# Triangle planes stored by halves of the picture, T loaded for two tiles in one DMA of 128 partitions, and the turned picture kept in bands

## The chip, the core and the metric

The kernel runs on one core of a Trainium2 chip. TensorE (PE) multiplies matrices into PSUM, VectorE (DVE), ScalarE (ACT) and GpSimd (POOL) work elementwise, and SyncE (SP) issues DMAs between DRAM and SBUF (128 partitions); ScalarE issues some DMAs too. One DMA is spread over the core's 16 DMA engines. The metric is the device time of one execution in microseconds, as the median of several runs; lower is better.

## The reference

The input x is a picture of 192 x 192 pixels with 64 channels in f32. Four layers follow one another, each of this form:

```python
def _L1_conv_ref(z, mask, ...):
    x = _layernorm(z, ln_in_w, ln_in_b)                      # layer 3 has none
    a = m * sigmoid(x @ w_a_g + b_a_g) * (x @ w_a_p + b_a_p)
    b = m * sigmoid(x @ w_b_g + b_b_g) * (x @ w_b_p + b_b_p)
    t = jnp.einsum('bikc,bjkc->bijc', a, b)                  # layers 0 and 1
    t = _layernorm(t, ln_out_w, ln_out_b) @ w_o + b_o
    g = sigmoid(x @ w_g + b_g)
    return g * t
```

and `x = x + layer(_gn(x))` with a group norm (32 groups over the whole picture) each time. Layers 2 and 3 contract over the other axis, `einsum('bkjd,bkid->bijd', left, right)`. Layers 0 and 2 multiply by the gate before the output matrix, layers 1 and 3 after it. Layer 0's product is made in bf16, the others in f32.

## The kernel before

**Layout.** A tile is two rows of pixels of the upper half of the picture and two of the lower: partition 64h + c holds channel c of half h, 384 pixels on the free axis. There are 48 tiles (`TILES`), taken four at a time through rings of four slots (`RING`, `TURNS` = 12).

**Stage A** (`phase_a`) normalises each tile, projects it to left and right with their gates (L568, L578), and VectorE's `glu` writes the products to `lr`, which fills most of SBUF (L1062, L1069). The gate of the output goes to DRAM (`gate_scratch`, L342). For layers 1 and 3 the tiles come from `x_scratch` one by one (`load`, L309).

**Stage B1** (`phase_b1`) multiplies left by right for 64 channels, four channels a group (`GROUPS` = 16): row i of the plane T on PSUM partitions. ScalarE copies the first 128 rows of a group to SBUF (`main`, L846) and issues their store (L850); VectorE copies the other 64 (`tail`, L1113) and SP stores them in two DMAs (L380). T lies in DRAM as `t_scratch` [64 channels][192 x 192 pixels] (`t_scratch_bf16` in layer 0). Between the tails SP loads residual tiles into parts of `lr` that are free (L370), in layers 1 to 3 after a wait for ScalarE's copy. A slot of `plane_out` is used again after four groups, when `planes_stored` has counted its three DMAs.

**Stage B2** (`phase_b2`) reads T back. `load_t` brings two tiles of both halves into `in_ring`, in two DMAs of 64 partitions and 192 KB (96 KB in layer 0), L405; `centre` (L678) waits for both. Two pairs of tiles are in the ring; a new pair is issued when the two tiles of its slots have been centred (`b2_z`). Variance (L693), spreading of the deviation (L702), the output matrix (L718), the bias and the residual (L1144, or L1150 and L1277) and the group norm's statistics (L1155) follow. At the start of the stage TensorE runs filler matmuls (`keep_clock`, L618), and in layer 0 two more ahead of each of the first four output matmuls.

**The turn.** Layers 2 and 3 work on the transposed picture. At the end of layer 1 ScalarE writes each new tile transposed into `turned`, part of `lr` (L889). When all 48 are there, the whole is written to `turned_scratch` [half h][half h2][channel][96 j][96 i]: SP writes the first 8 of 96 rows j of each of the four blocks (L453, `EARLY` = 4 tiles), ScalarE the other 88 (L926), a partition's rows being 3 KB and 33 KB long without a break. SP waits for its four and then gathers the first tiles of layer 2 (`gather`, L316): one DMA of 128 partitions for each half h, for two tiles. SP keeps each gathered pair in `x_scratch` (`keep`, L321) for the residual. The second round of gathers waits for ScalarE's four DMAs (`turned_stored[1]`), for the slots to be used and for the kept pair to have landed. VectorE waits for all eight before it writes to `lr`.

**Order.** All orders are written out by hand: each engine runs its own program, and semaphores are the only ties. DMAs of a queue are issued in the order of that engine's code, and a wait in it holds back whatever stands behind it.

## Time and profile before

| | us |
|---|---|
| median of three runs | 1471.77 (1465.33 to 1473.02) |
| the profiled execution | 1468.82 |
| its span, first to last instruction | 1466.6 |

| stage | layer 0 | layer 1 | layer 2 | layer 3 |
|---|---|---|---|---|
| first gate matmul of A (L550) | 54.5 | 399.0 | 815.1 | 1163.9 |
| first and last product matmul of B1 (L636) | 246.4 to 271.2 | 576.7 to 642.0 | 975.8 to 1038.7 | 1289.7 to 1352.1 |
| first and last centring matmul of B2 (L678) | 280.4 to 373.1 | 652.2 to 746.9 | 1048.7 to 1146.2 | 1361.7 to 1455.1 |

(Starts in us from the first instruction; the last product matmul of L636 is within a us of the end of B1.) Over the span PE is busy 87%, DVE 69%, ACT 64%, POOL 36%. The times of the profile are those of one execution. A busy share is an average over stages that have different limits, so the stages are read one by one: which wait ends last there. A row of waits tells who waited, for whom, how long in all, how often, and the longest; a DMA has an issue (a time on the queue of SP, SPq, or of ScalarE, ACTq) and a landing, some us later.

### The profile page before, as it was taken

To read this page: it belongs to the slowest core of one execution; us is meant where nothing else is said; L and a number is where in the kernel's file an instruction comes from. 1 tells how busy PE (TensorE), PEld (TensorE's weight loads), DVE (VectorE), ACT (ScalarE), POOL (GpSimd) and SP (SyncE) were. 2 spreads that over 40 slices of the span, in tenths; PEclk is the share of its full clock that TensorE was granted. 3 is DMA by queue.
4 is the path that set the end of the run, shared out by engine and by line. 5 is a ranking of instruction groups with operands and counts; after the bars stand their busy time and mean duration, and the time that the engine had idled before them with its cause. 6 is when DMAs were issued, how large, how long until landed. Compare 5 with 4: busy or idle time off the path is not lost. (4 is left out here: it accounts for less than half of the span.)

```text
span 1466.6 us, 43428 instructions
## 1 busy us (share of the span) xinstructions
PE 1268.9 (87%) x12854; PEld 769.3 (52%) x12854; DVE 1006.8 (69%) x2880; ACT 932.2 (64%) x2045; POOL 528.5 (36%) x490
## 2 busy tenths in 40 slices
PE   0799998899799998999950999999899788899898
PEld 0455554577454544765530555557555343467564
DVE  6577776388699996219970788852299899921687
ACT  0577775599577774229960788851499677722675
POOL 0355552045455553004530666630055300000355
PEclk9999999999899999999985999999999899999999
DMA  8011113578433332986659455549799544469797
GB/s 286 22 50 52 50 48 97 154 221 253 155 109 107 107 112 73 285 270 188 193 147 222 153 185 165 176 136 299 243 277 282 182 154 150 145 208 312 236 300 251
DMA packets 219684, 258.74 MB, mean 176 GB/s; under 512 B 53984, under 2 KB 208992, under 8 KB 219360
## 3 DMA queue, kind: packets, MB, share of 16 engines
q1 hardware_dynamic: 185504, 227.18, 49.9%
q10 hardware_dynamic: 34112, 30.68, 7.4%
q8 instruction: 40, 0.66, 0.2%
q14 instruction: 28, 0.23, 0.1%
HBM read 139.83 MB, written 117.96 MB: 176 GB/s over the span
## 5 line engine op out<-in xcount | busy, mean ns | idle before, releaser
L1062 DVE SCALAR_TENSOR_TENSOR lr<-ps,mask,act_out 128x128 f32 (+5 forms) x1152 | 278.8, 310 | 52.9 <-ACT act_out L805 46.5
L1232 POOL TENSOR_TENSOR rstd<-ve,half_col 128x6 f32<-128x6 f32 x144 | 190.3, 1322 | 254.8 <-DVE ve L1029 221.1
L1277 POOL TENSOR_TENSOR new_ring<-val,lr 128x384 f32<-128x384 f32 x96 | 103.4, 1077 | 386.6 <-issue 303.1
L568 PE MATMUL ps<-w_parts,val 64*128 64x256 bf16 (+1 forms) x1728 | 199.1, 309 | 18.9 <-DVE lr L1062 18.1
L805 ACT ACTIVATE act_out<-ps 128x384 f32<-128x384 f32 x384 | 176.0, 483 | 50.3 <-PE ps L578 34.1
L1265 POOL TENSOR_TENSOR val<-act_out,gate_ring 128x384 f32<-128x384 f32 x96 | 103.6, 1080 | 225.1 <-ACT act_out L882 186.0
L781 ACT ACTIVATE cen<-ps,gn 128x384 f32<-128x384 f32 x144 | 83.8, 582 | 102.0 <-PE ps L523 99.6
L859 ACT ACTIVATE cen<-ps 128x384 f32<-128x384 f32 x192 | 108.5, 565 | 61.9 <-PE ps L678 61.6
L678 PE MATMUL ps<-in_ring,k 128*128 128x384 f32 x288 | 130.3, 536 | 17.5 <-DMA in_ring<-t_scratch 17.2
L1113 DVE COPY cen<-ps 128x384 f32<-128x384 f32 x48 | 26.8, 558 | 160.6 <-PE ps L636 160.6
L636 PE MATMUL ps<-lr 64*128 64x192 f32 (+3 forms) x896 | 125.5, 330 | 8.8 <-DVE lr L1062 5.2
L1239 POOL TENSOR_TENSOR rb<-rstd,one_col 128x384 f32<-128x384 f32 x144 | 128.8, 894 | 11.3
L523 PE MATMUL ps<-in_ring,w_centre 128*128 128x384 f32 x192 | 92.7, 571 | 42.9 <-issue 42.7
L568 PEld LDWEIGHTS ps<-w_parts,val 64*128 64x128 bf16 (+1 forms) x1728 | 79.2, 114 | 78.0 <-DVE lr L1062 40.9
L636 PEld LDWEIGHTS ps<-lr 64*128 64x128 f32 (+3 forms) x896 | 103.9, 179 | 27.7 <-issue 17.5
L874 ACT ACTIVATE rb<-rstd 128x384 f32<-128x384 f32 x192 | 114.4, 596 | 3.8 <-DVE rstd L1123 3.8
L1024 DVE TENSOR_TENSOR sq_low<-sq 128x384 bf16<-128x384 f32 x144 | 79.5, 552 | 54.1 <-ACT sq L783 54.1
L814 ACT ACTIVATE val<-xn 128x384 bf16<-128x384 f32 (+1 forms) x144 | 75.3, 523 | 64.8 <-PE ps L578 42.6
L797 ACT ACTIVATE gate_ring<-ps,gate_bias 128x384 f32<-128x384 f32 x192 | 111.2, 579 | 5.8 <-PE ps L550 5.5
L1132 DVE TENSOR_TENSOR xn<-ps,cen 128x384 f32<-128x384 f32 x192 | 104.4, 544 | 15.0 <-PE ps L702 12.4
L861 ACT ACTIVATE sq<-ps 128x384 f32<-128x384 f32 x192 | 106.7, 556 | 0.0
L578 PE MATMUL ps<-w_parts,val 64*64 64x128 bf16 (+1 forms) x3456 | 105.5, 235 | 0.0
(112 smaller groups left out, 2595.5 us busy)
## 6 DMA issues: line engine op xcount, KB each, us to landing
gate_scratch<-gate_ring SPq DMA_DIRECT2D x192, 192.0 KB, 2.3
gate_ring<-gate_scratch SPq DMA_DIRECT2D x96, 384.0 KB, 3.7
lr<-x_scratch SPq DMA_DIRECT2D x72, 384.0 KB, 5.1
in_ring<-t_scratch SPq DMA_DIRECT2D x144, 192.0 KB, 3.4
x_scratch<-new_ring SPq DMA_DIRECT2D x48, 384.0 KB, 3.2
in_ring<-x_scratch SPq DMA_DIRECT2D x96, 192.0 KB, 2.4
lr<-x SPq DMA_DIRECT2D x6, 1536.0 KB, 15.9
t_scratch<-cen SPq DMA_DIRECT2D x96, 96.0 KB, 4.0
```

The lines of the kernel that those rows point to most:

```text
L568: mm = nc.tensor.matmul(banks[h][:, :, 0:P], moving(x, s)[half(h), N * r:N * r + P], proj_weights(w, h)[:, 0:2 * P], start=start, stop=sto ...
L578: mm = nc.tensor.matmul(banks[h][TAIL * e:TAIL * e + TAIL, :, P:COLS], moving(x, s)[half(h), N * r + P:N * r + N], proj_weights(w, h)[:, 2 ...
L636: mm = nc.tensor.matmul(ps[:, b + i % 2, N * (i // 2):N * (i // 2) + N], left[:, 0:P], right, start=first and i < 2, stop=last and i >= 2, ...
L678: nc.tensor.matmul(ps[:, s % 2, 0:TILE], w_c, t_slots(l, s)[:, 0, :], start=True, stop=True).then_inc(b2_z, 1)
L797: nc.scalar.activation(gate_ring[:, s, :], ps[:, 3, 0:TILE], ACT.Sigmoid, bias=gate_bias[:, 0:1])\
L805: nc.scalar.activation(act_out[:, r, :].rearrange("p (h c) -> p h c", h=2), ps[:, 4 + 2 * r:6 + 2 * r, COLS:2 * COLS], ACT.Sigmoid).then_i ...
L859: nc.scalar.activation(cen[:, s, :], ps[:, s % 2, 0:TILE], ACT.Copy, scale=T_SCALE[l])\
L861: nc.scalar.activation(sq[:, s % 2, :], ps[:, s % 2, 0:TILE], ACT.Square, scale=T_SCALE[l])\
L874: nc.scalar.activation(rb[:, s % 2, :].rearrange("p (a c) -> p a c", c=C), rstd[:, s % 2, :].rearrange("p (a o) -> p a o", o=1) .broadcast ...
L1062: ins = nc.vector.scalar_tensor_tensor(out5[:, h, lo // 2:hi // 2, :, m], ps[:, 4 + 2 * r + h, lo:hi].rearrange("p (a e) -> p a e", e=2), ...
L1232: nc.gpsimd.tensor_tensor(rstd[:, s % 2, :], ve[:, s % 2, :], half_col[:, :], ALU.pow)\
L1239: nc.gpsimd.tensor_tensor(rb[:, s % 2, :].rearrange("p (a c) -> p a c", c=C), rstd[:, s % 2, :].rearrange("p (a o) -> p a o", o=1) .broadc ...
```

## The change

- T's planes lie in DRAM by halves of the picture: `t_scratch` is now [2][64 channels][96 x 192 pixels]. Half and channel together are 128 rows of equal distance, so `load_t` is one DMA of 128 partitions and 384 KB.
- A group's plane is stored in four DMAs: ScalarE stores rows 0 to 95 (96 partitions), SP the tail as before and then, after a wait for ScalarE's copy (now in every layer and group), rows 96 to 127 (32 partitions).
- The turned picture lies in DRAM in 24 bands of 8 rows j: [band][128 partitions][8 x 96], 3 KB per partition and band. SP stores the first band of each half h2 (2 DMAs of 128 partitions), ScalarE the other 11 of each (2 DMAs). A gather of two tiles is four DMAs of 64 partitions.
- In layer 0's B2 the two `keep_clock` matmuls ahead of each of the first four output matmuls are gone.
- Counts of semaphores follow.

```diff
--- before.py
+++ after.py
@@ -36,7 +36,8 @@
 TURNS = TILES // RING
 PAIRS = RING // 2
 PIECES = 6
-EARLY = 4
+BAND = 2 * RING
+BANDS = HALF // BAND
 SUBS = ROWS * TILES
 GROUP = 4
 GROUPS = C // GROUP
@@ -61,9 +62,9 @@
 def build_triangle_layers(nc, x_in, params, consts, mask3_k, mask3_row, x_out):
     scratch = nc.dram_tensor("x_scratch", [TILES, P, TILE], F32).ap()
     gate_dram = nc.dram_tensor("gate_scratch", [TILES, P, TILE], F32).ap()
-    turned_dram = nc.dram_tensor("turned_scratch", [2, 2, C, HALF, HALF], F32).ap()
-    t_f32 = nc.dram_tensor("t_scratch", [C, N * N], F32).ap()
-    t_bf16 = nc.dram_tensor("t_scratch_bf16", [C, N * N], BF16).ap()
+    turned_dram = nc.dram_tensor("turned_scratch", [2 * BANDS, P, BAND * HALF], F32).ap()
+    t_f32 = nc.dram_tensor("t_scratch", [2, C, HALF * N], F32).ap()
+    t_bf16 = nc.dram_tensor("t_scratch_bf16", [2, C, HALF * N], BF16).ap()
 
     with ExitStack() as ctx:
         def sb(name, shape, dt=F32):
@@ -184,10 +185,10 @@
         turned = lr[:, N * HALF:2 * N * HALF].rearrange("p (j i) -> p j i", i=HALF)
 
 
-        def turned_rows(h, h2, first, behind):
-
-            return (turned_dram[h, h2, :, first:behind, :],
-                    turned[C * h:C * h + C, HALF * h2 + first:HALF * h2 + behind, :])
+        def turned_bands(first, count):
+
+            bands = turned.rearrange("p (b j) i -> p b (j i)", j=BAND)
+            return (turned_dram.rearrange("b p f -> p b f")[:, first:first + count, :], bands[:, first:first + count, :])
 
         x_all = lr[:, COLS * N // 2:].rearrange("p (t f) -> p t f", f=TILE)
 
@@ -196,7 +197,7 @@
 
         def t_tiles(l, n):
 
-            return t_dram(l).rearrange("c (h t f) -> h c t f", h=2, f=TILE)[:, :, bass.ds(n, 2), :]
+            return t_dram(l).rearrange("h c (t f) -> (h c) t f", f=TILE)[:, bass.ds(n, 2), :]
 
         slots = lr[:, :].rearrange("p (a f) -> p a f", f=TILE)
 
@@ -233,15 +234,15 @@
 
         def plane_dram(l):
 
-            return t_dram(l).rearrange("(g d) (i j) -> g i d j", d=GROUP, j=N)
+            return t_dram(l).rearrange("h (g d) (i j) -> g h i d j", d=GROUP, j=N)
 
         def planes_count(l, g):
 
-            return 48 * (l * (GROUPS // RING) + g // RING)
+            return 64 * (l * (GROUPS // RING) + g // RING)
 
         def in_count(l, s=0):
 
-            return 16 * TURNS * ((l > 1) + (l > 2) * (2 if s % 2 == 0 else 0))
+            return 16 * TURNS * ((l > 1) + (l > 2) * (4 if s % 2 == 0 else 0))
 
         n_params = [4 + HAS_LN[l] + (1 if l < 2 else (2 if HAS_MASK[l] else 0)) for l in range(LAYERS)]
 
@@ -308,16 +309,18 @@
                 def load(n, s):
                     sp.dma_start(in_ring[:, s, :], src[n, :, :]).then_inc(in_loaded[s], 16)
 
-                def gather(n, s):
+                def gather(band, s):
 
                     for h in range(2):
-                        rows = turned_dram[h].rearrange("h2 c j i -> (h2 c) j i")[:, bass.ds(ROWS * n, 2 * ROWS), :]
-                        slot = in_ring[:, s:s + 2, :].rearrange("p a (r i) -> p (a r) i", r=ROWS)
-                        sp.dma_start(slot[:, :, HALF * h:HALF * h + HALF], rows).then_inc(in_loaded[s], 16)
+                        for h2 in range(2):
+                            rows = turned_dram[bass.ds(BANDS * h2 + band, 1), C * h:C * h + C, ROWS * HALF * s:ROWS * HALF * (s + 2)]
+                            slot = in_ring[C * h2:C * h2 + C, s:s + 2, :].rearrange("p a (r i) -> p (a r) i", r=ROWS)
+                            sp.dma_start(slot[:, :, HALF * h:HALF * h + HALF],
+                                         rows.rearrange("b p (r i) -> p (b r) i", i=HALF)).then_inc(in_loaded[s], 16)
 
                 def keep(n, i, s):
 
-                    sp.wait_ge(in_loaded[s], in_count(l) + 32 * (i + 1))
+                    sp.wait_ge(in_loaded[s], in_count(l) + 64 * (i + 1))
                     sp.dma_start(two_tiles(scratch, n), in_ring[:, s:s + 2, :]).then_inc(natural_stored[s // 2], 16)
 
                 def step_gathering(n, i, s, ahead):
@@ -325,7 +328,7 @@
 
                         sp.wait_ge(used, l * TILES + n + lead + 1)
                         sp.wait_ge(natural_stored[s // 2], 16 * (i + 2))
-                        gather(n + lead + RING - 1, s - 1)
+                        gather(i + 2, s - 1)
                     sp.wait_ge(a_gate, l * TILES + n + 1)
                     sp.dma_start(gate_dram[n, :, :], gate_ring[:, s, :]).then_inc(gate_stored[s], 16)
                     if s % 2 and ahead >= RING + 1:
@@ -343,15 +346,15 @@
 
                 if l == 2:
                     for n in range(0, RING, 2):
-                        gather(n, n)
+                        gather(0, n)
                     for n in range(0, RING, 2):
                         keep(n, 0, n)
 
-                    sp.wait_ge(turned_stored[1], 16 * 4)
+                    sp.wait_ge(turned_stored[1], 16 * 2)
                     for n in range(0, RING, 2):
                         sp.wait_ge(used, l * TILES + n + 2)
                         sp.wait_ge(natural_stored[n // 2], 16)
-                        gather(RING + n, n)
+                        gather(1, n)
                     keep(RING, 1, 0)
                     over_tiles(sp, step_gathering, 2 * RING)
                     return
@@ -374,14 +377,13 @@
 
                 dram = plane_dram(l)
                 for g in range(GROUPS):
-                    _, tail = plane_out(l, g)
+                    main, tail = plane_out(l, g)
                     sp.wait_ge(b1_tail, l * GROUPS + g + 1)
                     for e in range(2):
-                        sp.dma_start(dram[g, P:N, e::2, :], tail[TAIL * e:TAIL * e + TAIL, :, :])\
+                        sp.dma_start(dram[g, 1, P - HALF:HALF, e::2, :], tail[TAIL * e:TAIL * e + TAIL, :, :])\
                             .then_inc(planes_stored[g % RING], 16)
-                    if l and g < LATE:
-
-                        sp.wait_ge(b1_main, l * GROUPS + g + 1)
+                    sp.wait_ge(b1_main, l * GROUPS + g + 1)
+                    sp.dma_start(dram[g, 1, 0:P - HALF, :, :], main[HALF:P, :, :]).then_inc(planes_stored[g % RING], 16)
                     if l == 2 and g == 0:
                         for pair in range(PAIRS):
                             sp.wait_ge(natural_stored[pair], 16 * TURNS)
@@ -401,9 +403,7 @@
                     sp.wait_ge(planes_stored[s], planes_count(l + 1, s))
 
                 def load_t(n, s):
-                    for h in range(2):
-                        sp.dma_start(t_slots(l, s, 2)[C * h:C * h + C, :, :], t_tiles(l, n)[h, :, :, :])\
-                            .then_inc(t_loaded[s // 2], 16)
+                    sp.dma_start(t_slots(l, s, 2), t_tiles(l, n)).then_inc(t_loaded[s // 2], 16)
 
                 def gate_used(n):
 
@@ -449,9 +449,8 @@
                     sp.wait_ge(b2_turned, TILES)
 
                     for h2 in range(2):
-                        for h in range(2):
-                            sp.dma_start(*turned_rows(h, h2, 0, ROWS * EARLY)).then_inc(turned_stored[0], 16)
-                    sp.wait_ge(turned_stored[0], 16 * 4)
+                        sp.dma_start(*turned_bands(BANDS * h2, 1)).then_inc(turned_stored[0], 16)
+                    sp.wait_ge(turned_stored[0], 16 * 2)
                 else:
                     stores = sum(1 for m in range(l + 1) if m != 1)
                     for s in range(PAIRS):
@@ -515,7 +514,7 @@
                 def centre(n, i, s):
                     if l == 2:
 
-                        pe.wait_ge(in_loaded[s // 2 * 2], in_count(l) + 32 * (i + 1))
+                        pe.wait_ge(in_loaded[s // 2 * 2], in_count(l) + 64 * (i + 1))
                     elif l:
                         pe.wait_ge(in_loaded[s], in_count(l) + 16 * (i + 1))
                     slot_free(pe, a_sq, base + n - 1)
@@ -673,7 +672,7 @@
                 w_c = centre_bf[:, :] if l == 0 else k_centre
 
                 def centre(n, i, s):
-                    pe.wait_ge(t_loaded[s // 2], 32 * (l * TURNS + i + 1))
+                    pe.wait_ge(t_loaded[s // 2], 16 * (l * TURNS + i + 1))
                     slot_free(pe, b2_sq, base + n - 1)
                     nc.tensor.matmul(ps[:, s % 2, 0:TILE], w_c, t_slots(l, s)[:, 0, :],
                                      start=True, stop=True).then_inc(b2_z, 1)
@@ -713,8 +712,6 @@
                         slot_free(pe, b2_new, base + n - 1)
                     else:
                         slot_free(pe, b2_gated, gated_before(l) + n - 1)
-                    if l == 0 and isinstance(n, int) and n < RING:
-                        keep_clock(4 + s % 2, 2)
                     nc.tensor.matmul(ps[:, 4 + s % 2, 0:TILE], w_out_s[:, l % 2, :],
                                      (val if GATE_FIRST[l] else xn)[:, s % 2, :], start=True, stop=True)\
                         .then_inc(b2_out, 1)
@@ -847,7 +844,7 @@
                                          ps[:, b:b + 2, 0:2 * N].rearrange("p e (a q) -> p e a q", q=N),
                                          ACT.Copy).then_inc(b1_main, 1)
                     act.wait_ge(b1_main, l * GROUPS + g + 1)
-                    act.dma_start(plane_dram(l)[g, 0:P, :, :], main).then_inc(planes_stored[g % RING], 16)
+                    act.dma_start(plane_dram(l)[g, 0, :, :, :], main[0:HALF, :, :]).then_inc(planes_stored[g % RING], 16)
 
             def phase_b2(l):
                 base = l * TILES
@@ -922,8 +919,7 @@
 
                     act.wait_ge(b2_turned, TILES)
                     for h2 in range(2):
-                        for h in range(2):
-                            act.dma_start(*turned_rows(h, h2, ROWS * EARLY, HALF)).then_inc(turned_stored[1], 16)
+                        act.dma_start(*turned_bands(BANDS * h2 + 1, BANDS - 1)).then_inc(turned_stored[1], 16)
 
             for l in range(LAYERS):
                 phase_a(l)
@@ -1096,7 +1092,7 @@
                 if l == 2:
 
                     for part in range(2):
-                        dve.wait_ge(turned_stored[part], 16 * 4)
+                        dve.wait_ge(turned_stored[part], 16 * 2)
                 over_tiles(dve, step)
                 glu(TILES - 1, 1)
 
```

SP at the turn from layer 1 to layer 2, from its stores of the turned picture on. Before:

```order
L453 DMA turned_scratch<-lr 64x768 x4
L316 DMA in_ring<-turned_scratch 128x4x96 x4
L321 DMA x_scratch<-in_ring 128x2x384 x2
L316 DMA in_ring<-turned_scratch 128x4x96 x4
L321 DMA x_scratch<-in_ring 128x2x384
L330 DMA gate_scratch<-gate_ring 128x384
L316 DMA in_ring<-turned_scratch 128x4x96 x2
L330 DMA gate_scratch<-gate_ring 128x384
```

The same place now:

```order
L452 DMA turned_scratch<-lr 128x768 x2
L318 DMA in_ring<-turned_scratch 64x4x96 x8
L324 DMA x_scratch<-in_ring 128x2x384 x2
L318 DMA in_ring<-turned_scratch 64x4x96 x8
L324 DMA x_scratch<-in_ring 128x2x384
L333 DMA gate_scratch<-gate_ring 128x384
L318 DMA in_ring<-turned_scratch 64x4x96 x4
L333 DMA gate_scratch<-gate_ring 128x384
```

Two stores stand where four stood, and twice as many gathers of half as many partitions; ScalarE's four stores of `64x8448` are two of `128x11x768` in the same place of its program.

SP at the end of layer 2's B1 and the start of its B2 (`cen` holds the tails, `xn` and `act_out` the main part of the last two groups). Before:

```order
L380 DMA t_scratch<-cen 64x2x192 x2
L370 DMA lr<-x_scratch 128x2x384 x2
L380 DMA t_scratch<-cen 64x2x192 x4
L405 DMA in_ring<-t_scratch 64x768 x4
L370 DMA lr<-x_scratch 128x2x384 x3
L405 DMA in_ring<-t_scratch 64x768 x6
L367 DMA gate_ring<-gate_scratch 128x2x384
L443 DMA x_scratch<-new_ring 128x2x384
```

The same place now:

```order
L383 DMA t_scratch<-cen 64x2x192 x2
L386 DMA t_scratch<-in_ring 32x4x192
L373 DMA lr<-x_scratch 128x2x384 x2
L383 DMA t_scratch<-cen 64x2x192 x2
L386 DMA t_scratch<-xn 32x4x192
L383 DMA t_scratch<-cen 64x2x192 x2
L386 DMA t_scratch<-act_out 32x4x192
L406 DMA in_ring<-t_scratch 128x768 x2
L373 DMA lr<-x_scratch 128x2x384 x3
L406 DMA in_ring<-t_scratch 128x768 x3
L370 DMA gate_ring<-gate_scratch 128x2x384
L443 DMA x_scratch<-new_ring 128x2x384
```

A store of 32 partitions follows each pair of tails, the last of them right ahead of the first load of T, and the loads of T are half as many.

## Rows read from the trace of the kernel before

**Rows 1.** Instructions in order of time at the turn: start, length, engine, line.
```profile
757.45 5.77 SPq L453 DMA_DIRECT2D turned_scratch<-lr  x4
...
798.05 5.65 SPq L316 DMA_DIRECT2D in_ring<-turned_scratch  x4
...
804.95 2.90 PE L523 MATMUL ps<-in_ring,w_centre 128*128 128x384 f32 x4 [42.69 <-issue]
...
809.77 2.91 PE L523 MATMUL ps<-in_ring,w_centre 128*128 128x384 f32 x4
...
815.12 0.66 PE L550 MATMUL ps<-val,w_gate_parts 128*128 128x384 bf16 x3 [0.24 <-DVE val L1046]
...
817.36 0.91 PE L523 MATMUL ps<-in_ring,w_centre 128*128 128x384 f32 x2
```

**Rows 2.** Waits of SP's queue over the whole span: us in total, times, longest.
```profile
SPq L316 <- DMA turned_scratch<-lr: 34.8, 1, 34.8
```

**Rows 3.** Windows: bounds, length, then the columns that the first row names.
```profile
core 0: us, PE busy (x) PEld busy (x) DVE busy (x) ACT busy (x) POOL busy (x), PEclk, DMA share, GB/s
...
764.00:798.00 34.00, 0.00 (x0) 0.00 (x0) 0.00 (x0) 0.00 (x0) 0.00 (x0) 0.50 1.02 230
...
6.00:18.00 12.00, 2.69 (x6) 1.60 (x6) 6.74 (x18) 0.00 (x0) 0.00 (x0) 1.00 1.01 353
...
817.00:970.00 153.00, 147.07 (x2257) 86.15 (x2257) 130.79 (x273) 127.75 (x271) 104.69 (x91) 1.00 0.51 165
```

**Rows 4.** DMA from 757 to 806 us, and L926's stores, issue to landing.
```profile
DMA packets 2805, 10.32 MB, mean 211 GB/s; under 512 B 2236, under 2 KB 2292, under 8 KB 2548
...
DMA to landing us min/median/max: 13.9/28.5/41.2
```

**Rows 5.** Windows of B2's steady part, layers 0 to 3, columns as in rows 3.
```profile
290.00:382.00 92.00, 89.96 (x550) 66.50 (x549) 77.15 (x183) 85.43 (x219) 46.02 (x46) 1.00 0.76 230
660.00:754.00 94.00, 91.94 (x592) 50.90 (x590) 92.40 (x230) 92.31 (x225) 47.72 (x46) 1.00 0.61 180
1060.00:1155.00 95.00, 87.07 (x578) 53.38 (x579) 92.22 (x227) 87.81 (x221) 54.36 (x47) 1.00 0.86 266
1369.00:1461.00 92.00, 87.00 (x591) 54.74 (x591) 78.08 (x183) 64.70 (x179) 51.28 (x46) 1.00 0.90 277
```

**Rows 6.** Waits from 1358 to 1462 us, layer 3's B2.
```profile
PE ps L678 <- DMA in_ring<-t_scratch: 6.7, 9, 1.6
...
PEld ps L678 <- DMA in_ring<-t_scratch: 3.0, 2, 2.2
```

**Rows 7.** The chain that ended last, from layer 3's last tail: start, length, what.
```profile
1353.73 4.00 DMA t_scratch<-cen
...
1357.80 0.54 SPq L405
...
1358.38 3.29 DMA in_ring<-t_scratch
...
1363.82 5.12 DMA in_ring<-t_scratch
```

**Rows 8.** SP's gathers of layer 2: two in the loop, all, those of the gap.
```profile
841.50 0.98 SPq L316 DMA_DIRECT2D in_ring<-turned_scratch  x2
...
848.47 0.97 SPq L316 DMA_DIRECT2D in_ring<-turned_scratch  x2
...
DMA to landing us min/median/max: 2.5/2.7/6.3
...
in_ring<-turned_scratch SPq DMA_DIRECT2D x4, 192.0 KB, 4.3
```

**Rows 9.** Groups by line from 282 to 300 us: the fillers of layer 0.
```profile
L618 PE MATMUL ps<-k 128*128 128x384 f32 x20 | 7.6, 496 | 0.1
```

**Rows 10.** DMA issues from 1358 to 1466 us: count, KB each, median us to landing.
```profile
in_ring<-t_scratch SPq DMA_DIRECT2D x48, 192.0 KB, 3.7
...
gate_ring<-gate_scratch SPq DMA_DIRECT2D x22, 384.0 KB, 4.1
```

## Prediction

> **What bounds the kernel now.** I read the windows by stage first, then the waits and the chain inside the stages that the change touches, and last the instructions in order of time at the one long gap. Four layers run one after the other, each as stage A (projection), B1 (the triangle product) and B2 (the output). B1 and the steady part of A keep TensorE full: in layer 2's A it is busy 147.07 of 153 us [rows 3]. Nothing that only eases a DMA can help there.
>
> The steady part of B2 differs by layer [rows 5]. In layer 1 VectorE and ScalarE are both full (92.40 and 92.31 of 94 us) and the DMA engines are busy 0.61: transfers have no say. In layer 0 TensorE is full. In layer 2 VectorE has 92.22 of 95. In layer 3 nobody is full but the DMA engines (0.90 at 277 GB/s): TensorE has 87.00 of 92, and its waits for T in that stage are 6.7 + 3.0 us, once at the start of the stage and then where loads come late [rows 6].
>
> The gap is the turn of the picture between layers 1 and 2. SP and ScalarE start to write the transposed picture (9.44 MB) at 757.45 us; SP then sits 34.8 us in one wait for its own four small stores [rows 2] and reads the first band back at 798.05; TensorE starts at 804.95, the first gate matmul of layer 2 stands at 815.12 and the first load-dependent step of the second round of tiles at 817.36 [rows 1]. From 764 to 798 no engine does anything; TensorE's granted clock is 0.50 there, the 1.2 GHz level, after its last work near 762 [rows 3]; its centring matmuls at 804.95 take 0.73 us each and those at 817.36 0.46 [rows 1]. So the gap takes 815.1 - 757.5 = 57.6 us, and it is made of two things: the rate of the dump, and that the first band lands nearly last.
>
> **The dump (the large term).** Removed: four DMAs of SP (64 partitions, 3 KB rows) and four of ScalarE (64 partitions, 33 KB rows). Added: two of each queue with 128 partitions and 3 KB rows. Bytes are the same.
> - Rate. While the dump runs the DMA engines are busy all the time and move 230 GB/s (211 over 757 to 806), and ScalarE's last DMA lands 41.2 us after its issue [rows 3, 4]. The load of x at the start, 128 partitions a DMA, moves 353 GB/s with the engines just as busy [rows 3]. So it is not the engines' number that limits the dump. Three things differ: 64 against 128 partitions, 33 KB against 1.5 KB rows, and writing against reading DRAM. The change removes the first two. For writes the nearest row is layer 3's B2, a mixture of stores and of loads by 128 and 64 partitions: 277 GB/s at 0.90, or 308 with the engines full [rows 5]. Bounds: 211 (nothing gained) and 353 (reads only). I take 300, by that mixture.
> - The Trainium skill (SBUF — State Buffer, section "Door 1: The DMA port swizzle") says that partitions 0 to 63 reach only 8 of SBUF's 16 DMA ports, and that only one transfer over 128 partitions reaches all. The ratio of the two rows, 353/211 = 1.67, goes that way. By it alone the dump would come near the rate of the x load, and the sum below would be 7 us better; by the other reading (writes are slow) it would be 12 us worse.
> - Order. Before, SP's sixteen 3 KB rows per DMA engine finish when about as many of ScalarE's 33 KB rows have: SP's wait ends at 798, when the dump has some 7 us left [rows 1, 2]. The two queues are thus served row by row. Now ScalarE's rows are 3 KB too, and SP's share (16 of 192 rows on an engine) is through after twice its own bytes: 1.6 MB at 300 GB/s = 5 us, plus some 3 us to issue and to land. The first band is readable at about 766 instead of 798.
> - What is late next. SP then issues eight gathers (64 per DMA engine of 384 B rows for each pair of tiles) against the rest of the dump. Row by row, the first pair costs 64 of the dump's 3 KB rows with it: 64 x (3072 + 384) B x 16 engines = 3.5 MB = 12 us, landed about 778; the second pair about 790. The whole dump with these gathers is 9.44 + 0.79 MB = 10.2 MB, 34 us at 300, ended about 793 with its start and landing. Two things hang on that: VectorE may not write lr before it, and SP may not gather the second round before it.
> - Sum. The second pair at 790 gives the first gate matmul at 790 + (815.1 - 809.8, the same stretch of before) = 795.4; the second round is issued at 794 (eight issues instead of four) and lands at 799.5, which holds TensorE some 2 us, where its fifth tile was taken at 817.36 before. Layer 2 starts **817.4 - 799.5 = 18 us earlier**, I take 17. At 211 GB/s the dump ends near 808 and the second round lands near 812.5: 5 us. At 353 it is 24. The clock is at 0.50 in the gap in both kernels and comes back as long after the start: no term.
>
> **The gathers of layer 2.** 24 pairs of tiles now take 4 DMAs of 64 partitions where they took 2 of 128. SP's issues go from 0.98 to about 2.0 us per pair, in a period of 6.97 us (841.50 to 848.47), and the landing of 2.7 us [rows 8] may grow. The gather, its keep store and the gate stores of the same queue are behind it. A pair is issued two tiles before TensorE takes it, so 6.97 - 0.98 - 2.7 = 3.3 us are free and 1 us is spent: nothing, 0 to +3.
> - The same section of the Trainium skill speaks against this edit: each gather is now a transfer of half the ports. That would stretch the 2.7 us, and cost nothing while the 3.3 us last.
>
> **T in one load (B2 of all layers).** One DMA of 384 KB for two of 192 KB, 96 fewer issues. The second issue (0.54 to 0.60 us [rows 7]) goes from each load's latency; the landing of one 192 KB DMA is 3.7 us at the median in layer 3's B2 and a 384 KB load of the gate, 128 partitions, lands in 4.1 [rows 10]. So a load shortens from 0.5 + 0.6 + 3.7 to 0.5 + 4.1 us, near 0.2 to 1 us; and if the 64 partitions were the slow part here too, the DMA engines' 0.90 falls.
> - Layer 3: of 92 us TensorE has 5 free. Nearly all are waits that the loads end. I take -4; bounds 0 and -5, where TensorE is full.
> - Layer 2: VectorE has 92.2 of 95; -1, bounds 0 and -2.8. Layers 0 and 1: 0, other engines are full.
> - The fill at the start of each B2 is a chain of loads: 3.29, then after four tiles' room 5.12 us [rows 7]. Each loses an issue of 0.6 us: -1 per layer, -4 in all; bounds 0 and -6.
>
> **Planes by halves (B1).** ScalarE's main store shrinks from 128 to 96 partitions; SP stores the other 32 (one more issue of 0.6 us per group, 64 in all) after a wait for ScalarE's copy. The 16 groups take 62.5 us in layer 3 (the table of stages), 3.9 us each, and SP's queue has two tails, this store and at most two residual loads: at most 3 us. That is hidden behind TensorE until the last group. There SP's tail issue at 1353.73 is now followed by a third store, and the 4.00 us landing ends the chain [rows 7]: +0.5 per layer, +2 in all; bounds 0 and +4.
>
> **keep_clock in layer 0.** Eight filler matmuls go from the first four tiles; they are 16 of the 20 records (two for each) that are busy 7.6 us together [rows 9], so some 6 us of TensorE. TensorE's clock is 1.00 there. They stand in the fill, beside ScalarE's work: between -2 and, if the clock falls once as it does in other layers' fills, +3; I take +0.5.
>
> **Sum** against the profiled execution: 1468.8 - 17 - 4 - 1 - 4 + 2 + 0.5 = 1445.3. That execution is 3 us under the median of the runs shown (1471.8) and inside their spread; I forecast **1445**, 1.8% under the median.
>
> **Rivals.**
> - Writes stay slow (dump at 211 GB/s, 3 KB rows no better): boundary -5, the rest as above: 1457. For it: no row shows DRAM written fast alone. Against it: 308 GB/s by mixture.
> - The band lands with the dump in spite of its shorter rows, because ScalarE's 2816 rows are queued first: gathers then start at 793 and not at 766, the first pair lands at 797 against 804.9. Boundary -8: 1454.
> - Both sides good: dump at 353, all 5 us of layer 3: 1468.8 - 24 - 5 - 2 - 5 + 1 = 1434.
> - Slower: layer 2's gathers become the bound. At the gap SP's four gathers took 5.65 us, 1.4 each [rows 1]. If each of the four issues in the loop cost that, and a half-width gather landed in the 4.3 us of the gathers at the gap and not in 2.7 [rows 8], a pair would take 5.6 + 4.3 = 9.9 us where TensorE gives 6.97: +2.9 us over 22 pairs = 65 us, and with the rest 1445 + 65 = 1510. It decides from the point where issue and landing pass 6.97 us; the time is above before's from 8.2 us on. Against it: in the loop an issue takes 0.5 us.
> - It doesn't do what it says: T's loads are no faster by 128 partitions, since stores and gates fill the engines. Layers 2 and 3 then give 0: 1450, inside the range.
>
> **How the numbers follow.** Forecast (with the last rival) 0.66, slow writes 0.13, band with dump 0.07, both good 0.08, slower 0.06. The range 1434 to 1461 takes in all but the slower case and the worst ends. A change of under 0.5% (7 us, 1464.4) can't be told from none. Faster 0.88, same 0.07, slower 0.05.
>
> **What would show it.** Right: SP's wait after the band stores under 12 us; ScalarE's dump landing before 797; TensorE's first matmul of layer 2 near 778 to 785 and the first gate matmul near 795; over 280 GB/s in the dump; layer 3's waits for T under 5 us. Wrong: a dump still near 211 GB/s; TensorE idle before its centring matmuls in layer 2's loop; a later first load in every B2, which would mean that the third plane store costs more than it is given here.

## The result

The changed kernel takes **1504.5 us** (median of four executions, 1503.5 to 1505.3) against 1471.7 for the kernel before: a ratio of 1.023, interval 1.020 to 1.026. It is slower by 33 us where 27 us less were forecast. The profiled execution took 1505.09 us, its span 1502.9.

The granted clock tells where to look. The page of each kernel has it in 40 slices, in tenths of full speed; first before, then after:

```profile
PEclk9999999999899999999985999999999899999999
```

```profile
PEclk9999999855558999999999599999999989999999
```

The short low in the middle (the turn) has shrunk as forecast. But four slices are new: 297 to 444 us, which is layer 0's B2. Windows of after show it (bounds, length, busy us of PE, PEld, DVE, ACT, POOL with counts, clock, DMA share, GB/s), then layer 2's and layer 3's B2:

```profile
297.00:440.00 143.00, 143.00 (x518) 113.19 (x518) 79.10 (x173) 94.79 (x215) 43.81 (x44) 0.50 0.47 145
...
1100.00:1197.00 97.00, 86.66 (x577) 52.48 (x576) 91.57 (x226) 87.58 (x221) 54.34 (x47) 1.00 0.83 259
...
1411.00:1497.00 86.00, 85.48 (x590) 54.11 (x590) 78.13 (x184) 64.88 (x180) 50.84 (x46) 1.00 0.90 296
```

TensorE is busy for all of layer 0's B2, yet at a granted clock of 0.50. Its output matmuls take 847 ns each in place of 489, and 48 tiles take 150 us in place of 92 (the first of [rows 5]). The rows of the line groups, before and after:

```profile
L718 PE MATMUL ps<-val,w_out_s 128*128 128x384 f32 x95 | 38.8, 489 | 1.1 <-POOL val L1265 1.1
```

```profile
L715 PE MATMUL ps<-val,w_out_s 128*128 128x384 f32 x84 | 62.5, 847 | 0.0
```

The turn, in order of time, answers to [rows 1]:

```profile
820.71 0.83 SPq L452 DMA_DIRECT2D turned_scratch<-lr  x2
827.78 10.72 SPq L318 DMA_DIRECT2D in_ring<-turned_scratch  x8
...
842.26 2.90 PE L522 MATMUL ps<-in_ring,w_centre 128*128 128x384 f32 x4 [16.73 <-issue]
...
853.58 1.14 PE L549 MATMUL ps<-val,w_gate_parts 128*128 128x384 bf16 x3 [0.36 <-DVE val L1042]
```

From the first store to the first gate matmul it is 32.9 us where it was 57.6. This stretch repeats well: it is 32.7 to 32.9 us in all ten traces of kernels that store bands by 128 partitions, and 57.4 in e2 below, which turns as before does. SP's wait is 6.2 us [rows 2], ScalarE's last store lands 26.5 us after its issue [rows 4], and in mid-dump the DMA engines move 392 GB/s where they moved 230 [rows 3]:

```profile
SPq L318 <- DMA turned_scratch<-lr: 6.2, 1, 6.2
```

```profile
DMA to landing us min/median/max: 15.0/20.8/26.5
```

```profile
825.00:835.00 10.00, 0.53 (x2) 0.44 (x2) 0.24 (x2) 0.00 (x0) 0.00 (x0) 0.50 1.03 392
```

Stage by stage, the lag of after behind before (from the first and last instructions of each stage, one execution of each):

| place | lag, us | what was added or taken |
|---|---|---|
| layer 0, last product matmul of B1 | 1.9 | +1.9 |
| layer 0, first centring matmul of B2 | 6.4 | +4.5 |
| layer 0, last output matmul | 63.4 | +57.0, the clock |
| layer 1, last output matmul | 63.2 | -0.2 |
| layer 2, first gate matmul | 38.5 | -24.7, the turn |
| layer 2, last product matmul | 40.0 | +1.5 |
| layer 2, last output matmul | 42.5 | +2.5 |
| layer 3, first centring matmul | 42.7 | +0.2 |
| layer 3, last output matmul | 36.4 | -6.3 |

### The profile page after: what moved, and what is told of

Same layout as the page of the kernel before. It is cut to its first block and busy times, and to the rows that moved or that the text cites. A ratio compares the mean times of both kernels' runs of the same rounds, so it can differ in the third digit from the quotient of the medians.

```text
span 1502.9 us, 43336 instructions
## 1 busy us (share of the span) xinstructions
PE 1330.4 (89%) x12838; PEld 820.9 (55%) x12838; DVE 1011.4 (67%) x2880; ACT 943.4 (63%) x2045; POOL 528.4 (35%) x490
## 5 line engine op out<-in xcount | busy, mean ns | idle before, releaser
L856 ACT ACTIVATE cen<-ps 128x384 f32<-128x384 f32 x192 | 104.9, 546 | 62.2 <-PE ps L677 58.7
L701 PE MATMUL ps<-k,rb 128*128 128x128 f32 x576 | 113.2, 312 | 4.6 <-ACT rb L871 4.0
L701 PEld LDWEIGHTS ps<-k,rb 128*128 128x128 f32 x576 | 81.1, 158 | 65.3 <-ACT rb L871 28.7
L871 ACT ACTIVATE rb<-rstd 128x384 f32<-128x384 f32 x192 | 110.3, 575 | 3.8 <-DVE rstd L1119 3.8
L715 PE MATMUL ps<-val,w_out_s 128*128 128x384 f32 x192 | 108.8, 659 | 1.7 <-POOL val L1261 1.5
```

The lines of the kernel that those rows point to most:

```text
L701: mm = nc.tensor.transpose(ps[:, 2 + s % 2, P * j:P * j + P], rb[:, s % 2, P * j:P * j + P], k_ident)
L715: nc.tensor.matmul(ps[:, 4 + s % 2, 0:TILE], w_out_s[:, l % 2, :], (val if GATE_FIRST[l] else xn)[:, s % 2, :], start=True, stop=True)\
L856: nc.scalar.activation(cen[:, s, :], ps[:, s % 2, 0:TILE], ACT.Copy, scale=T_SCALE[l])\
L871: nc.scalar.activation(rb[:, s % 2, :].rearrange("p (a c) -> p a c", c=C), rstd[:, s % 2, :].rearrange("p (a o) -> p a o", o=1) .broadcast ...
```

## The experiments

The theory after this comparison: all else came out near the forecast, and the eight filler matmuls that the change took out of layer 0's B2 are worth 57 us (K). The rival (G): the plane stores put an idle stretch of TensorE ahead of that stage, and this is what lets the clock fall.

**e1: the fillers put back into the changed kernel.**

```diff
+                    if l == 0 and isinstance(n, int) and n < RING:
+                        keep_clock(4 + s % 2, 2)
                     nc.tensor.matmul(ps[:, 4 + s % 2, 0:TILE], w_out_s[:, l % 2, :],
```

> The changed kernel with the eight keep_clock matmuls of layer 0's B2 put back. Theory K: their absence is what leaves TensorE at a granted clock of 0.50 from 297 to 444 us, so with them the clock is 1.00 there, the output matmuls of layer 0's B2 run over some 92 us and not 150, and the time is 1504 - 57 = 1447 us (1442 to 1454). Rival G: the 4 us in which TensorE stands idle ahead of B2 (SP's late plane stores) are what sends the clock down, and fillers four tiles later don't help: over 1490.

Measured: 1446.3 us, ratio to before 0.984 (0.980 to 0.988). A window of layer 0's B2:

```profile
298.00:388.00 90.00, 88.52 (x547) 65.95 (x546) 75.60 (x180) 84.41 (x217) 45.04 (x45) 1.00 0.75 233
```

The clock is 1.00 and the output matmuls run over 91.9 us. The same late plane stores are in it, and layer 0's B2 starts as late as in after (286.6 against 286.8), so G alone doesn't do it. But the fillers do not keep the clock from falling. Right ahead of that window it is down in e1 too, as in after from 297.3 on:

```profile
294.80:298.20 3.40, 3.32 (x8) 1.83 (x6) 0.67 (x2) 2.14 (x6) 1.30 (x2) 0.51 0.41 101
```

In e1 it is back at 1.00 from 298.2, behind the first two fillers; in after, where the fillers are missing, it comes back at 444. So what the fillers change is how long the low lasts. G seems to have a part in the fall itself, as far as one trace of each kernel tells. With the planes of layer 0 in halves the clock fell there (294.8 to 297.3) in five traces of six: after, e1, e4, e5 and e8, not in e10. With the old planes and the fillers it fell between the start of that B2 and its last output matmul in one of seven (e11, twice for 3.4 us), not in before, e3, e6, e7, e9 and e12. e2 below, with the old planes and without the fillers, has it too (292.5).

**e2: the kernel before with only those fillers taken out.**

```diff
-                    if l == 0 and isinstance(n, int) and n < RING:
-                        keep_clock(4 + s % 2, 2)
```

> The kernel before with only the eight keep_clock matmuls of layer 0's B2 taken out; layout, stores and loads as before. Theory K: the clock falls to 0.50 soon after the fill of layer 0's B2 and stays there, and the time is 1472 + 50 to 57 = 1522 to 1529 us. Rival G: without the idle time ahead of B2 nothing happens, 1468 to 1473 us.

Measured: four executions at 1531.4, 1530.2, 1524.6 and 1463.1 us. Its profile (of the first) shows the same stage as after:

```profile
298.00:440.00 142.00, 142.00 (x510) 111.93 (x509) 79.25 (x173) 93.07 (x209) 42.86 (x43) 0.50 0.46 143
```

Nothing else was touched, so the fillers' absence is enough. But one execution of four escaped, and then ran at 1463, like the kernel before: without the fillers this stage takes one of two courses. Of the fast one only the mean clock is known, 0.966 like the kernel before's, where the others have 0.915 to 0.920; whether the clock stayed up in that stage or fell for a moment is not. This also makes the median of e2 (1527) a number that says less than its four parts; the same is not true of after, whose four executions agree within 2 us.

**e3: the kernel before with only the bands** (the diff above without the planes, `load_t` and `keep_clock` hunks).

> The kernel before with only the turned picture in bands (two stores of 128 partitions in each queue, gathers as four DMAs of 64 partitions). Theory: the turn alone gives what it gave in the changed kernel, first gate matmul of layer 2 at 32.9 us after the first store and not 57.6, with layer 2's loop 1 to 2 us longer: 1472 - 23 = 1449 us (1446 to 1453). Rival: a part of the 25 us comes from another edit, and the time is above 1455.

Measured: 1445.7 us (3 less than expected), ratio 0.984 (0.980 to 0.988). First store to first gate matmul 754.2 to 787.0, 32.8 us. The bands alone give what e1 gives; so the halves of T, with all that belongs to them, sum to nothing: what layer 3 gains (below), layer 0 loses.

**e4: e1 with both main stores issued by ScalarE.**

```diff
-                    sp.wait_ge(b1_main, l * GROUPS + g + 1)
-                    sp.dma_start(dram[g, 1, 0:P - HALF, :, :], main[HALF:P, :, :])...
+                    if l and g < LATE:
+                        sp.wait_ge(b1_main, l * GROUPS + g + 1)
...
                     act.dma_start(plane_dram(l)[g, 0, :, :, :], main[0:HALF, :, :])...
+                    act.dma_start(plane_dram(l)[g, 1, 0:P - HALF, :, :], main[HALF:P, :, :])...
```

> e1 with the store of rows 96 to 127 of each group issued by ScalarE right behind its own, and not by SP; SP waits for ScalarE's copy only where the kernel before did. Theory: in layer 0 a group of B1 lasts 1.6 us while SP's three stores take 1.8 us to issue, which put the start of B2 6.4 us later; with two on SP and two on ScalarE the 6.4 us come back: 5 to 7 us faster than e1, 1440 to 1442 us. Rival: the stores' number or their width sets the end of B1 and not SP's queue: within 2 us of e1.

Measured: 1442.8 us, 3.5 less than e1, but not where it was expected: layer 0's B1 ends at 275.4 (e1: 273.4) and its B2 starts at 287.8 (286.6). In this kernel the order of time of ScalarE at the end of that B1 reads:

```profile
273.35 0.81 ACT L845 ACTIVATE in_ring<-ps 128x768 bf16<-128x768 f32 x1 [1.21 <-PE ps L635]
274.19 0.32 ACTq L849 DMA_DIRECT2D t_scratch_bf<-in_ring  x1
274.54 2.18 ACTq L850 DMA_DIRECT2D t_scratch_bf<-in_ring  x1
276.82 0.81 ACT L845 ACTIVATE xn<-ps 128x768 bf16<-128x768 f32 x1 [2.66 <-issue]
```

Now ScalarE's own issues (0.32 + 0.5 us and more) stand between its copies. The groups of layer 0 are so short (1.6 us) that the fourth store is late in either queue. That fits the time of issue as the cause, with a wrong cure; but e4's rival, the number or the width of the stores, forecast the same start of B2, and nothing here parts the two. Where the 3.5 us came from was not found (the two profiled executions differ by 1.5 us).

**e5: e1 with the dump by 64 partitions**, bands and 3 KB rows as they are.

```diff
-                        sp.dma_start(*turned_bands(BANDS * h2, 1))...
+                        for h in range(2):
+                            sp.dma_start(*turned_bands(BANDS * h2, 1, h))...
```

(and the same in ScalarE's queue; `h` picks 64 of the 128 partitions on both sides)

> e1 (the changed kernel with the fillers) with the turned picture stored in the same bands of 3 KB rows but by DMAs of 64 partitions, four in each queue in place of two. Theory W (width): the 64 partitions set the rate; the dump goes back from 392 to some 200 to 230 GB/s, its last store lands some 45 us after the start and not 27, and the gap (first store to first gate matmul) grows from 33 to 45 to 52 us. Rival L (row length): the 33 KB rows were the slow thing; the rate stays over 350 GB/s and the gap within 3 us of 33.

Measured: one execution, 1465.6 us. A window in mid-dump:

```profile
770.00:790.00 20.00, 0.38 (x2) 0.29 (x2) 0.16 (x1) 0.00 (x0) 0.00 (x0) 0.50 0.99 242
```

**e7: the kernel before with the dump by 128 partitions and its old rows** (33 KB on ScalarE's queue).

```diff
-    turned_dram[h, h2, :, first:behind, :], turned[C * h:C * h + C, ...]      # x2 for h
+    turned_dram[h2].rearrange("h c j i -> (h c) j i")[:, first:behind, :], turned[:, ...]
```

> The kernel before with the turned picture stored by DMAs of 128 partitions (two in each queue) but with its old rows: 3 KB on SP's queue, 33 KB on ScalarE's; gathers by four DMAs of 64 partitions as in the changed kernel. Theory W: the dump moves over 350 GB/s all the same. If the two queues are served row by row, SP's two stores land only with the dump's end, 20 to 26 us after their issue where the changed kernel has 4.7, so the gap is between: 38 to 45 us against 57.6 and 33; time 1455 to 1460 us. Rival L: 211 GB/s stays, the gap over 52 us.

Measured: one execution, 1449.6 us, 5 less than the least expected (the gap, 37.9 us, is at the low end of what was). The window in mid-dump, then the landing of SP's two stores:

```profile
757.00:777.00 20.00, 1.33 (x5) 1.07 (x5) 1.26 (x7) 0.00 (x0) 0.56 (x1) 0.50 0.97 413
```

```profile
DMA to landing us min/median/max: 11.8/17.1/22.3
```

e5 and e7 with before and e3 make a square. First store to first gate matmul of layer 2, us (rate in mid-dump):

| | 33 KB rows | 3 KB rows |
|---|---|---|
| 64 partitions | 57.6 (230 GB/s) | 51.6 (242) |
| 128 partitions | 37.9 (413) | 32.8 (398) |

Width is worth 19 to 20 us at either row length; short rows are worth 5 to 6 at either width. One corner is not clean: before gathers by 128 partitions in two DMAs, the other three by 64 in four. So the rate is the width's, and what the short rows give is the order: with them SP's stores land 4.7 us after issue at the median, with long rows 17.1, as in a service row by row. The Trainium skill (SBUF — State Buffer, "Door 1: The DMA port swizzle") has partitions 0 to 63 on half the ports. The ratios here, 413 to 230 (1.8) and 398 to 242 (1.6), go that way and stay under two.

**e6: e1 with layer 0's T as before**, the rest in halves (the edit in outline).

```diff
+                    if l == 0:
+                        continue          # SP: no third store; ScalarE stores all 128 rows
...
+                    if l == 0:            # load_t: two DMAs of 64 partitions, old layout
```

> e1 with layer 0's T as the kernel before has it (one plane store of 128 partitions by ScalarE, two tails by SP, loads by two DMAs of 64 partitions); bands, and halves for layers 1 to 3, stay. Theory: the 5 us that B2 of layer 0 starts later in e1 come from SP's third store in groups of 1.6 us; they come back: 1440 to 1442 us, against 1446.3 of e1. Rival: they are chance or belong to another edit: within 2 us of e1.

Measured: 1437.4 us (1435.6 to 1445.4), ratio to before 0.978 (0.975 to 0.981). That is 9 us under e1, more than expected. Layer 0's B1 ends at 268.0 and its B2 starts at 278.2, 8 us earlier than in e1; but 2.5 of the 8 are already there at the first product matmul (244.2 against 246.7), up to which the two kernels are the same. From the first product matmul to the start of B2 it is 34.0 us in e6 and in before, 39.9 in e1, 40.5 in after and 41.7 in e4: the old planes give 6 us back. The other 3 us are not explained.

**e8: the changed kernel with one filler ahead of every fourth output matmul.**

```diff
+                    if l == 0 and s == 0:
+                        keep_clock(4 + s % 2, 1)
```

> The changed kernel (no fillers ahead of the first four output matmuls) with one filler matmul ahead of every fourth output matmul of layer 0's B2, 12 in all. If a little more matmul work all along is enough, the clock is 1.00 in layer 0's B2 and the time is within 5 us of e1 (1446). If what counts is the stretch right after the start of B2, where eight fillers stood in e1 and one stands now, the clock falls there, and one filler in four tiles doesn't bring it back: 1500 to 1515 us.

Measured: five executions, 1457.9, 1440.0, 1442.0, 1444.0 and 1448.8 us: neither answer. The profile is of the slowest, two windows of layer 0's B2:

```profile
297.00:326.00 29.00, 29.00 (x101) 22.38 (x100) 14.68 (x32) 18.10 (x41) 7.99 (x8) 0.50 0.42 132
328.00:400.00 72.00, 70.91 (x447) 54.45 (x445) 63.47 (x148) 69.61 (x176) 36.77 (x38) 1.00 0.75 233
```

The clock falls at 296 as in after, but comes back at 327, where in after it stayed down to the end of the stage. One filler in four tiles doesn't keep it up for sure. In the one execution that was traced the clock came back right behind the third of them (324.2 to 325.7); the other four, at 1440 to 1449 us, can't have stayed low either.

**e10: T loaded in two DMAs cut by tile**, 128 partitions each.

```diff
-                    sp.dma_start(t_slots(l, s, 2), t_tiles(l, n))...
+                    for a in range(2):
+                        sp.dma_start(t_slots(l, s, 2)[:, a, :], t_tiles(l, n)[:, a, :])...
```

> e1 with T loaded in two DMAs again, but cut by tile (128 partitions, 192 KB, rows of 1.5 KB) and not by half of the picture (64 partitions). In layer 3's B2, first to last output matmul takes 87.7 us in e1 and 91.9 in the kernels that load by halves. Theory W (width): the 64 partitions cost it, so 87 to 89 us here. Rival N (number): the second issue and completion cost it, so 91 to 93 us.

Measured: one execution, 1441.4 us; in layer 3, 87.1 us from first to last output matmul. That is width again, not the number of issues. TensorE's waits for T in layer 3's B2, in after (see [rows 6] for before):

```profile
PEld ps L677 <- DMA in_ring<-t_scratch: 2.2, 1, 2.2
...
PE ps L677 <- DMA in_ring<-t_scratch: 1.5, 1, 1.5
```

In layer 2 the same stretch is 93.0 us, where e1 has 96.5, after 98.0 and before 95.4. Over all kept traces it is 93.0 in the two with loads by tile, 94.9 to 95.8 in the four with loads by halves, and 94.8 to 98.0 in the eight with one load. An earlier start of the first tile is not the reason: in e10 `centre` waits for both loads of the pair (a count of 32), as before. The pair is there sooner: in layer 2's B2 a load by tile lands 3.0 us after its issue at the median, and the second is issued 0.35 us behind the first, where one load of 384 KB takes 4.0 us in e1 and 4.6 in after, and TensorE's waits for T there are 3.2 us in e10, 6.5 in e1 and 8.1 in after. Why two loads land sooner than one was not tested.

**e9, e11, e12: towards the best.** e9 is e6 with ScalarE issuing the fourth store in layers 1 to 3; e11 adds `elif l == 0 and s == 0: keep_clock(4, 1)` behind e9's fillers; e12 is e9 with e10's loads in layers 1 to 3.

> e6 with the stores of rows 96 to 127 in layers 1 to 3 issued by ScalarE behind its own. In those layers a group of B1 lasts 3.9 us and neither queue is short, so only the end of B1 can gain, some 0.6 us a layer: 1434 to 1437 us, against 1437.4 of e6. Rival: nothing, as SP's third store already lands with the tails.

> e9 with one more filler matmul ahead of every fourth output matmul in the rest of layer 0's B2. In e9 the clock stays up there in most executions, and ScalarE is the full engine of that stage, so 11 matmuls of 0.65 us should cost 0 to 2 us where the clock is up already. The median within 2 us of e9, and no execution that is 20 us or more above the others.

> e9 with T of layers 1 to 3 loaded by tile (two DMAs of 128 partitions and 192 KB) as in e10. In e10 layer 2's B2 took 93.0 us from first to last output matmul where e1 had 96.5, and layer 3's was as in e1: 3 to 4 us faster than e9, 1434 to 1436 us. Rival: e10's 3.5 us in layer 2 are chance between executions: within 1.5 us of e9 (1438.9).

Measured: e9 1438.9 (1432.0 to 1439.8), e11 1438.8 (1435.5 to 1443.1), e12 1436.0 (1435.8 to 1439.8), with ratios to before of 0.979, 0.978 and 0.977. e9 brought nothing that can be told from e6; e11's fillers cost nothing that the medians show (its traced execution took 94.0 us for layer 0's output matmuls, with the two short lows, where e9's took 91.7), and no execution of either kernel was out of line, so they were not needed in these either. In e12 layer 2's B2 is 93.0 us again, as in e10, but the medians of e6, e9 and e12 differ by less than their intervals allow to order. All three beat the kernel before by 2.1 to 2.3%; only e12's interval lies wholly beyond 2%.

## Why the prediction was wrong

- **The fillers of layer 0: the step that failed.** I priced their removal at -2 to +3 us, and the row behind it was that TensorE's clock is 1.00 in that stage and that other layers' lows are short. That row shows the clock with the fillers; it can't show what happens without them. Measured: +57 us in that stage and +58 in the whole time (after against e1), and +53 to +60 in three of e2's four executions. I did price a fall, at +3 us, as long as the lows in other layers' fills. Those were short, the matmul work behind them raised the clock again; without the fillers the work of layer 0's B2 doesn't, and with them a low at the same place lasts 3.4 us (e1). Once the clock is down TensorE is the bound of every tile, is busy all the time by its records, and the clock stays at 0.50 for 147 us. The Trainium skill (TensorE: Matmul & The Clock Gate, "Part 1: The HAM clock gate") says that "the default state is throttled, and activity releases the throttle". Here 143 of 143 us busy by the records did not release it.
- **The forecast without that step.** With the fillers back the kernel takes 1446.3 us; the sum was 1445.3. That is partly luck, since three terms were off and cancelled.
- **The turn: right, and under-sized.** Taken -17, measured -24.7 at the first gate matmul and -23.3 at the fifth tile, where the forecast had taken it: the value of the best bound. The mechanism holds in each part: the first pair was used 21.5 us after the first store (20.5 in the forecast), SP's wait was 6.2 us, the order is row by row. The term mis-sized was the rate: I took 300 GB/s from a mixture of stores and half-width loads; full-width stores with a few gathers move 398 (e1, e3). The mixture was held down by half-width loads only in part: with T's loads at full width the same stage moves 296 GB/s at 0.90 in after, 329 with the engines full where it was 308. The slow-writes rival is excluded by e5 and e7: wide writes at 413 are no slower than the x load's 353. That the clock comes back as long after the start in both kernels was wrong: it was up again 8 us behind the first centring matmul in before and 15 us behind it in after, which still has gate matmuls of 1.14 us for 0.66; the -24.7 contains that.
- **The planes: mis-sized.** Taken +2 over four layers, hidden in B1. For layers 1 to 3 it holds (lag +0.2 at the start of layer 3's B2). In layer 0 I used layer 3's 3.9 us for a group; its groups are in bf16 and take 1.6 us, less than the three stores on SP's queue take to issue. It cost 6.4 us there in after, and e6 gets 6 back. In after SP's queue at that place shows it, one group of 1.9 us after the other:

```profile
276.25 1.24 SPq L383 DMA_DIRECT2D t_scratch_bf<-cen  x2
277.54 0.59 SPq L386 DMA_DIRECT2D t_scratch_bf<-in_ring  x1
278.18 1.25 SPq L383 DMA_DIRECT2D t_scratch_bf<-cen  x2
279.47 0.59 SPq L386 DMA_DIRECT2D t_scratch_bf<-xn  x1
```

- **T in one load.** Layer 3: taken -4, measured from first to last output matmul -5.5 in after and -4.2 in e1; the waits for T went from 9.7 to 3.7 us, and the cause is width (e10). Layer 2: taken -1, measured +2.5 in after and +1.1 in e1; two full-width loads by tile turn it into -2.4 (e10, e12), the reason is open. The fills: taken -1 each, measured 0 to -1.
- **The gathers: right.** Layer 2 is 1.5 us longer from its first gate matmul to the end of its B1 (225.1 us for 223.6), but so it is in e2, which gathers as before does (225.1). The slower rival did not happen. Its issues do cost more than I said: 0.60 us each at the median, 2.6 us per pair of tiles, and the 3.3 us of room took it.
- **The rivals.** None was the case that came. The one that ended slower named another place, layer 2's gathers; that its 1510 us lies near the 1504.5 measured is chance.

## What stays open

Why three of e2's four executions fell into the low clock and one didn't, and why all four of after did, is not settled. After has one thing more than e2, TensorE idle for 4 us ahead of the stage; e1 has it too, and there the clock falls and comes back. What of the fillers brings it back, and which of the eight are needed, was not tried; e8 shows that one ahead of every fourth tile can do, after a longer low.

## What to carry to other kernels

Work that only keeps TensorE's clock up can't be priced from a profile in which it is up: before it is taken out, or while anything ahead of it is moved, ask what happens to the stage if the clock is 0.50 all along, and run it several times. A transfer between SBUF and DRAM that is cut should be cut along the free axis, by tile, and not into halves of the partitions. And the issue time of a queue is to be held against the shortest stage that uses the code, not against the one whose rows were at hand.

## What the runs showed of the hardware

- At the turn, stores of 128 partitions (with the first gathers among them) moved 392 to 413 GB/s, of 64 partitions 230 to 242, with the DMA engines busy 0.97 to 1.04 in all of them, whatever the row length (3 KB or 33 KB).
- The granted clock can stay at 0.50 while TensorE's records show it busy 143 of 143 us (small f32 and bf16 matmuls with weight loads between); with a filler matmul of 128 x 384 in f32 ahead of every fourth tile it was back after 31 us (e8), with two ahead of each of the first four tiles after 3.4 us (e1, e4, e5).
- Issuing a DMA took longer for 64 or 32 partitions than for 128 or 96. In layer 2's loop of gathers the issue was 395 ns at the median by 128 partitions and is 600 by 64:

```profile
L316 SPq DMA_DIRECT2D in_ring<-turned_scratch x48: 368/395/4133, 798.0 to 950.8; - x48
```

```profile
L318 SPq DMA_DIRECT2D in_ring<-turned_scratch x96: 595/600/1407, 827.8 to 994.0; - x96
```

  T's loads went from 492 to 345 ns; that is not their size, as e10's, with the old 192 KB each by 128 partitions, take 346. The plane stores of layer 0 take 0.32 to 0.38 us on ScalarE's queue by 96 partitions and 0.59 on SP's by 32; in e4, with both on ScalarE's queue, 0.32 to 0.35 and 0.51 to 0.73 at the median. So halving the partitions of a DMA doubled the count of issues and made each one longer. Why the issue takes longer was not tested.
